# Three sublayers of a perceiver stack: first self attention as two interleaved chains, inverse merges spread over later fills, cross attention values as block diagonal products

## The reference, cut to what matters

```
# sublayer 1, L0_attn: 16 heads of 8; rotary q and k; a cascade over the heads
s[h]   = q[h] @ k[h].T / sqrt(8) + causal
s[h]  += cascade_w[h-1] * mean over the queries of att[h-1]      # h > 0
att[h] = softmax(s[h]);   out = concat(att[h] @ v[h]) @ Wproj

# sublayer 4, L1_attn: a gated delta recurrence, 16 heads of 64, per-channel
# decays a and aR, learned beta and gamma, output clipped, then Wo

# sublayer 9, L3_xattn: q from x; k, v from the context; causal over (32, 257)
lin(x, W, b, A, B) = x @ W.T + b + x @ A.T @ B.T / 16
att = softmax(q @ k.T / sqrt(8) masked to s <= t);  out = lin(att @ v, Wp, bp, Ap, Bp)
```

## Time and profile before

| what | value |
|---|---|
| median of three runs | 3740.51 us (3736.25 to 3745.74) |
| the profiled execution, its own time | 3746.5 us |
| its span, first to last instruction | 3744.7 us, granted clock 0.833 |
| TensorE (PE) busy | 2824.1 us (75%), 50001 matmul records |
| VectorE (DVE) busy | 2288.9 us (61%) |
| ScalarE (ACT), GpSimd (POOL) busy | 1433.9 us (38%), 606.6 us (16%) |

### The profile page before, as it was taken

The page is one execution under the profiler, slowest core; times in us unless marked ns, Lnnn a source line. Parts: engine busy times, 40 slices in busy tenths (PEclk is TensorE's granted clock), DMA queues, the critical chain, the costliest instruction groups (busy, mean ns, idle before and its releaser), DMA issues. The chain is left out here.

```text
span 3744.7 us, 117402 instructions
## 1 busy us (share of the span) xinstructions
PE 2824.1 (75%) x50001; PEld 1980.9 (53%) x50009; DVE 2288.9 (61%) x5777; ACT 1433.9 (38%) x3268; POOL 606.6 (16%) x623
## 2 busy tenths in 40 slices
PE   8852347899995687878787877759998998696654
PEld 5510136444444566666666666536665665384443
DVE  3466532556546887778877887247776555564451
ACT  4312123334333343444444443426665333363220
POOL 0040032455540000000000000000000322061014
PEclk9865567899996698989988998959998998796575
DMA  2100023111101000000000000000001001251013
GB/s 81 40 0 0 0 95 111 55 37 44 43 20 44 3 4 3 4 3 4 4 4 3 4 4 4 3 10 24 24 24 42 0 0 29 71 121 44 5 35 96
DMA packets 69034, 107.01 MB, mean 29 GB/s; under 512 B 10384, under 2 KB 55072, under 8 KB 68032
## 3 DMA queue, kind: packets, MB, share of 16 engines
q1 hardware_dynamic: 56912, 78.25, 6.8%
q0 software_dynamic: 11696, 22.40, 2.4%
HBM read 87.97 MB, written 16.51 MB: 28 GB/s over the span
## 5 line engine op out<-in xcount | busy, mean ns | idle before, releaser
L2885 PE MATMUL psum<-l1d_rw,l1d_cols 64*32 64x32 f32 (+2 forms) x20480 | 246.0, 221 | 115.0 <-issue 71.2
L2394 POOL TENSOR_TENSOR l2x_qx<-l2x_q,consts 128x128 f32<-128x128 f32 x64 | 25.5, 398 | 1723.2 <-DVE l2x_q L2565 1399.5
L2885 PEld LDWEIGHTS psum<-l1d_rw,l1d_cols 64*32 64x32 f32 x20480 | 215.9, 110 | 160.8 <-issue 109.6
L2319 POOL TENSOR_SCALAR l1xs_p<-l1xs_p,l1xs_col 128x257 f32<-128x257 f32 x256 | 238.1, 932 | 243.3 <-DVE l1xs_col L2282 242.7
L2247 ACT ACTIVATE l1xs_p<-psum,l1xs_col 128x257 f32<-128x257 f32 x256 | 122.2, 477 | 256.1 <-DVE l1xs_col L2277 255.9
L2682 ACT COPY l1d_ya<-psum 128x512 f32<-128x512 f32 x160 | 94.2, 589 | 264.4 <-PE psum L2924 264.4
L2277 DVE TENSOR_REDUCE l1xs_col<-psum 128x1 f32<-128x257 f32 x256 | 107.3, 419 | 138.5 <-PE psum L2199 138.5
L3119 DVE TENSOR_TENSOR l1d_rw<-l1d_rw,l1d_tots 128x512 f32<-128x512 f32 x240 | 152.5, 685 | 26.7 <-PE psum L2885 24.9
L2199 PE MATMUL psum<-l1xs_keys,l1xs_qx 128*32 128x257 f32 x2048 | 161.8, 396 | 3.7 <-ACT l1xs_p L2247 3.7
L2211 PE MATMUL psum<-l1xs_pt,l1xs_vals 32*128 32x512 f32 x1152 | 162.0, 637 | 1.3 <-DVE l1xs_pt L2289 1.3
L2824 PE MATMUL psum<-l1d_src,l1d_wp 128*128 128x128 f32 x1024 | 144.2, 300 | 23.3 <-ACT l1d_src L2687 23.3
(11 more groups left out here) (562 smaller groups left out, 7121.1 us busy)
## 6 DMA issues: line engine op xcount, KB each, us to landing
l2f_w<-in_l2f_w SPq DMA_DIRECT2D x16, 768.0 KB, 4.7
l1xs_vals<-in_ctx_strips SPq DMA_DIRECT2D x16, 576.0 KB, 3.8
l0x_ctxT<-in_ctxT SPq DMA_DIRECT2D x16, 516.0 KB, 3.7
l1xs_keys<-in_ctxT SPq DMA_DIRECT2D x16, 516.0 KB, 3.5
l2x_ctxT<-in_ctxT SPq DMA_DIRECT2D x64, 129.0 KB, 2.1
l1d_wp<-in_l1d_wp SPq DMA_DIRECT2D x1, 2048.0 KB, 8.0
l2f_acc<-l2f_zero SPq DMA_DIRECT2D x8, 256.0 KB, 4.5
l2f_sums<-l2f_acc SPq DMA_DIRECT2D x8, 256.0 KB, 5.1
```

The costliest lines, as they stand in the source:

```text
L2319: nc.gpsimd.tensor_scalar(p[:, t % 4, :S2], p[:, t % 4, :S2], col[:, 2, t % 4:t % 4 + 1], None, ALU.mult).then_inc(s["norm"], 1)
L2885: mm = nc.tensor.matmul(k.ps[bank0 + pr + e // per * 2][b * T:b * T + T, e % per * w:(e % per + 1) * w], cols[rr, n, e * 128 + b * T:e * 1 ...
```

## The change

Sublayer 1 becomes one block without loops. The scores are made as in sublayer 9 (16 small products a bank, mask included), the values of a head as a block diagonal stationary tile of 128 rows by 32 columns (`vd`), so that one product does a sequence group. The 16 tiles are cut into two halves x = 0 and 1, each a chain of its own through the heads with instructions of 256 columns; transposes move from VectorE to TensorE; the output weights lie widened (`l0a_wp`, 1 MB instead of 64 KB) with four products per group of four heads. Sublayer 9 takes the same form of values, unit by unit (a unit is a bank of scores), and folds its output weights widened as well (16 more products ahead of the first chunk, 1 MB and 128 KB more to load). In sublayer 4 `turn` only writes the 16 entries that are needed, over a tile that is cleared once, and each merge stands one step later in the round. Computed is the same.

The diff, cut to its core (the old `small_scores` and `small_values` go as a whole):

```
-def small_scores(k, nm, w, scores, rotary, keys_from):
...
@@ -635,101 +427,269 @@
 
 def l0_attn(k):
...
+            def front(c):
+                src = k.XN[:, c * CH:(c + 1) * CH]
+                for n in range(2):
+                    if c > 0:
+                        pe.wait_ge(s["qk"], c * 2 - n)
+                    if c > 0 and n == 1:
+                        pe.wait_ge(s["vd"], c)
+                    for j in range(2):
+                        mm = nc.tensor.matmul(k.ps[pair(c, n) + j][:], wall[:, 2 * n + j, :], src, start=True, stop=True)
+                    mm.then_inc(s["p_mm"], 1)
+                pe.wait_ge(s["qk"], c * 2 + 1)
+                pe.wait_ge(s["group"], c + 1)
+                for b in range(TB):
...
+                                                  qk[r, c % 2, 0, n * T:(n + 1) * T],
+                                                  ks[r, c % 2, n].rearrange("p h s -> p (h s)"), start=False, stop=t == 3)
+                    mm.then_inc(s["sc_mm"], 1)
+
+            def turn(h, x):
+                pe.wait_ge(s["att"], h * 2 + x + 1)
+                if h < H - 1:
+                    nc.tensor.matmul(mean_ps[x][:, :half * T], k.const("meanT"),
+                                     att[:, x, h % 2].rearrange("p n s -> p (n s)"), start=True, stop=True
+                                     ).then_inc(s["mean_mm"], 1)
+                if h * 2 + x > 0:
+                    pe.wait_ge(s["t"], h * 2 + x)
+                for j in range(2):
+                    mm = nc.tensor.transpose(t_ps[:, j * 128:(j + 1) * 128],
+                                             att[:, x, h % 2, 4 * j:4 * j + 4].rearrange("p n s -> p (n s)"),
+                                             k.const("ident"))
+                mm.then_inc(s["t_mm"], 1)
+
+            def values(h, x):
+                pe.wait_ge(s["t"], h * 2 + x + 1)
+                if x == 0 and h % 4 == 0 and h > 0:
+                    pe.wait_ge(s["o"], h // 4)
+                m = slice(32 * (h % 4), 32 * (h % 4) + 32)
+                for j in range(2):
+                    for b in range(TB):
+                        n = (2 * x + j) * TB + b
+                        mm = nc.tensor.matmul(o_ps[m, n * T:(n + 1) * T], vd[:, n, h, :], attT[:, x, j, b * T:(b + 1) * T],
+                                              start=True, stop=True)
+                if x == 1 and h % 4 == 3:
+                    mm.then_inc(s["o_mm"], 1)
+
+            def out(g, t):
+                pe.wait_ge(s["o"], g + 1)
+                if g == 0:
+                    pe.wait_ge(s["kept"], 4 * NCH)
+                mm = nc.tensor.matmul(k.ps[t][:], wp[:, g, t, :], o[:, g % 2, :], start=g == 0, stop=g == 3)
+                if g == 3 or t == 3:
+                    mm.then_inc(s["out_mm"], 1)
+
+            front(0)
+            pe.wait_ge(s["set"], 2)
+            for c in range(1, NCH):
+                front(c)
+                scores(c - 1)
+            scores(NCH - 1)
+            pe.wait_ge(s["vd"], NCH)
+            for h in range(H):
+                turn(h, 0)
+                if h > 0:
+                    values(h - 1, 1)
+                turn(h, 1)
+                values(h, 0)
+                if h >= 4:
+                    out(h // 4 - 1, h % 4)
+            values(H - 1, 1)
+            for t in range(4):
...
+        @block.gpsimd
+        def _(pool):
+            for c in range(NCH):
+                tokens = k.XN[:, c * CH:(c + 1) * CH].rearrange("p (t b s) -> p b t s", t=4, b=TB)
+                nc.gpsimd.tensor_copy(xg[:, c].rearrange("p b (t s) -> p b t s", t=4), tokens).then_inc(s["group"], 1)
...
+            def first(h, x):
+                src = sc[:, h, half * x:half * x + half, :]
+                if h > 0:
+                    dve.wait_ge(s["mean_mm"], (h - 1) * 2 + x + 1)
+                    step(nc.vector.scalar_tensor_tensor(a[:, x].rearrange("p n s -> p (n s)"), mean_ps[x][:, :half * T],
+                                                     cw[:, h:h + 1], src.rearrange("p n s -> p (n s)"), ALU.mult, ALU.add))
+                    src = a[:, x]
+                else:
+                    dve.wait_ge(s["kept"], 8 * x + 8)
+                step(nc.vector.tensor_reduce(mx[:, x], src, AX.X, ALU.max))
+                nc.vector.tensor_tensor(a[:, x], src, spread(mx[:, x]), ALU.subtract).then_inc(s["shift"], 1)
+
+            def second(h, x):
+                dve.wait_ge(s["exp"], h * 2 + x + 1)
+                step(nc.vector.tensor_reduce(rs[:, x], a[:, x], AX.X, ALU.add))
+                step(nc.vector.reciprocal(rs[:, x], rs[:, x]))
+                if h >= 2:
+                    dve.wait_ge(s["t_mm"], (h - 2) * 2 + x + 1)
+                nc.vector.tensor_tensor(att[:, x, h % 2], a[:, x], spread(rs[:, x]), ALU.mult).then_inc(s["att"], 1)
+
...
+                rotate(c)
+            first(0, 0)
+            for h in range(H):
+                if h > 0:
+                    second(h - 1, 1)
+                second(h, 0)
+                first(h, 1)
+                if h + 1 < H:
+                    first(h + 1, 0)
+            second(H - 1, 1)
+            for t in range(4):
...
+            def values(u):
+                c, g = u // 4, u % 4
+                pe.wait_ge(s["at"], u + 1)
+                if g == 0:
+                    pe.wait_ge(s["vd"], c + 1)
                     if c > 0:
...
-                    mm.then_inc(s["own_mm"], 1)
+                        pe.wait_ge(s["o"], c)
+                    else:
+                        pe.wait_ge(s["bias"], 1)
+                for t in range(4):
+                    for h in range(4):
+                        mm = nc.tensor.matmul(o_ps[32 * h:32 * h + 32, g * 128 + t * T:g * 128 + t * T + T],
+                                              vd[:, c % 2, t, 4 * g + h, :], attT[:, u % 2, (t * 4 + h) * T:(t * 4 + h) * T + T],
+                                              start=True, stop=True)
+                mm.then_inc(s["o_mm"], 1)
 
             def out(c):
                 pe.wait_ge(s["o"], c + 1)
-                nc.tensor.matmul(out_ps[:], wf[:, 3, :], o[:], start=True, stop=True).then_inc(s["out_mm"], 1)
-
-            for j, n in enumerate((0, 1, 1, 2)):
+                if c == 0:
+                    pe.wait_ge(s["wide"], 4)
+                    pe.wait_ge(s["bias"], 1)
+                else:
+                    pe.wait_ge(s["x"], c)
+                pe.wait_ge(s["vd"], min(c + 3, NCH))
+                for b in range(TB):
+                    for g in range(4):
...
+                                              o[:, g, :], start=g == 0, stop=g == 3)
+                mm.then_inc(s["out_mm"], 1)
+
+            for j, n in enumerate((0, 1, 1)):
                 mm = nc.tensor.matmul(k.ps[0][:, j * D:(j + 1) * D], wa[:, n, :], wb[:, j, :], start=True, stop=True)
             mm.then_inc(s["fold_mm"], 1)
+            for g in range(4):
+                bank = k.ps[(1, 2, 3, 7)[g]]
+                for b in range(TB):
+                    mm = nc.tensor.matmul(bank[:, b * D:(b + 1) * D], wpa[:, g, b, :], wb[:, 3, :], start=True, stop=True)
+                mm.then_inc(s["wide_mm"], 1)
             pe.wait_ge(s["fold"], 1)
             front(0)
+            rows(0)
             pe.wait_ge(s["set"], 3)
-            for c in range(NCH):
-                scores(c)
-                if c + 1 < NCH:
+            scores(0)
+            pe.wait_ge(s["wide"], 4)
+            scores(1)
+            for g in range(4):
+                mm = nc.tensor.matmul(o_ps[:, :1], wp[:, g, 0, :], bv[:, g:g + 1], start=g == 0, stop=g == 3)
+            mm.then_inc(s["bias_mm"], 1)
+            for u in range(units):
+                c, g = u // 4, u % 4
+                if u + 2 < units:
+                    scores(u + 2)
+                if g == 0 and c + 1 < NCH:
                     front(c + 1)
-                if c > 0:
-                    values(c - 1)
+                if u > 0:
+                    values(u - 1)
+                if g == 1 and c + 1 < NCH:
+                    rows(c + 1)
+                if g == 2 and c > 0:
                     out(c - 1)
-            values(NCH - 1)
+            values(units - 1)
             out(NCH - 1)
...
             def turn(i):
 
                 dve.wait_ge(s["kc"], i + 1)
-                t = Steps(dve, s["turn"], i, 3)
+                t = Steps(dve, s["turn"], i, 2)
+                first = lambda x: x[:, T:T * T:2 * (T + 1)]
                 t(vc.transpose(lt[:, :T * T], kc[:]))
-                t(vc.tensor_scalar(xi[:, :T * T], lt[:, :T * T], -1.0, None, ALU.mult))
-                t(vc.memset(xi[:, 0:T * T:T + 1], 1.0))
+                t(vc.tensor_scalar(first(xi), first(lt), -1.0, None, ALU.mult))
 
             def merge(m):
...
             vc.memset(mr[:], 0.0)
-            vc.memset(ll[:], 0.0).then_inc(s["zero"], 1)
+            vc.memset(ll[:], 0.0)
+            vc.memset(xi[:], 0.0).then_inc(s["zero"], 1)
```

(15 more changed lines are left out.)

523 lines of the change are left out of this document (197 added, 326 removed).

## The result

The changed kernel takes 3516.4 us (median of 4 runs, 3514.4 to 3520.0) against 3743.1 for the kernel before: ratio 0.940, 95% interval 0.938 to 0.942. The forecast was 3556 with a range of 3512 to 3604. The sign, the three places and the order of the terms were right, and the time lies in the range, but not in the likeliest case's own range (3530 to 3580); the nearest case is rival B, 3511, though its parts came out otherwise, as the last sections show.

The account below looks back on a forecast made before the run. It took sublayer 1's heads as one chain, sublayer 4's wait for clip and TensorE's waits for instructions as the bounds; gains of 107 + 58 + 19 = 184 us from 3740.5 gave 3556 us, range 3512 to 3604.

Parts of the forecast that it names:

- the three places: Sublayers 1, 4 and 9 were to gain 107, 58 and 19 us.
- likeliest case: Whole kernel: the forecast itself, 3556 us, own range 3530 to 3580; chance 0.48.
- rival B: Fewer instruction waits or full clock in the heads: sublayers 1, 4, 9 give 130, 74, 25; 3511 us; chance 0.17.
- the order inside the heads: Sublayer 1: chain 0's mean stands behind the output product; chain 1's mean starts at 3.9, chain 0's next at 7.3 us.
- D: Sublayer 1's chains don't overlap: heads about 9.8 us, 37 us more than forecast, 3593 us; chance 0.1.
- what is late next is TensorE itself, and its instructions: Sublayer 4, once the wait for clip goes: 1.3 us a round given back.
- Rival C: Sublayer 4: the wait for clip turns into instruction waits, giving only 20 us; 3594 us; chance 0.2.
- rival E: Sublayer 4: the wait for clip was slack, so only sublayers 1 and 9 gain; 3604 us; chance 0.03.
- some 3 us go again for stretches at full clock: Sublayer 9: taken off the 111 us priced at half clock, giving 108 instead of 127.4.
- sublayer 9 with TensorE 75% busy got 0.55: Sublayer 9's old granted clock, used as evidence against full clock in rival B.
- The rule that fetching is hidden: Sublayer 4: instruction fetch mostly costs nothing, so nothing is given back; 16 us more gain, 3540 us.
- the prediction's own sign, 5 us: Prediction is wrong if a stretch other than the three sublayers moves by more than 5 us.

Follow-up runs that it names:

- run 1: The changed kernel with each output product of sublayer 1's heads issued one place earlier, between the two chains' means of the next head: 3512.7 us, ratio 0.937.
- Runs 5 and 6: run 5, and as 6 the kernel before with only merge_last(0) of sublayer 4 moved right behind clip: 3702.5 us, ratio 0.988.
- run 5: The kernel before with the shortened turn of sublayer 4 alone (16 entries negated instead of 1024, xi filled once): 3734.8 us, ratio 0.997.
- run 3: The changed kernel with sublayer 9's value products cut in four of 8 columns, neighbours in different strips of 32 array columns: 3564.8 us, ratio 0.951.
- run 4: The changed kernel with four stretches of small products that nothing reads put ahead of sublayer 9's folds: 3661.3 us in one profiled execution.
- run 2: The changed kernel with sublayer 9's value products cut in four of 8 columns, four in a row in the same strip: 3585.2 us, ratio 0.957.
- Run 9: run 1's edit plus sublayer 4's table load moved earlier, with TensorE's waits in sublayers 1 and 9 filled with products: 3504.3 us, ratio 0.937 to the kernel before.

## Why the prediction came out as it did

**Right: the three places, and the order inside the heads.** The heads of sublayer 1 came as far apart as forecast, and run 1 shows the cause by moving it. That the period was met to 0.2 us is in part luck, as its two halves were 0.7 too long and 0.5 too short. D is out: the chains overlap. Its price was also wrong: 16 heads at 9.8 us are 157, 50 more than 107 and not 37, which gives 3606, outside the range.

**Right: sublayer 4 waited for `clip`, and time would be given back.** 58 forecast, 54 the usual gain. Runs 5 and 6 put it on the two parts that the prediction named. The gain has the two parts that were forecast: between the two traces before and the six of the new code, TensorE's waits fell by some 36 us (54.8 for `clip` less what was given back), and its products, the same records, took some 22 us less, against 20 forecast for the half clock. The step that failed inside it is who gives back: "what is late next is TensorE itself, and its instructions". Late next was ScalarE with its table load (16.6 us), and `issue` grew by some 10 us in all, not by 18. So the size given back, 18 us, was right with half of its cause. Rival C, 20 us for this sublayer, is out, and by run 5 rival E too. Rival B's 74 is out as well, though the first trace had 68.

**Wrong: the clock in sublayer 9, 20 us.** The failing step is "some 3 us go again for stretches at full clock". With the prices of half clock the sublayer came to 111 us. In the trace the clock is 0.77, not 0.55, and TensorE's work of 75 us fits in 89. The argument against rival B, "sublayer 9 with TensorE 75% busy got 0.55", took the old clock for a property of the sublayer. It belonged to the old value products: run 3, with their old number, gives 32 of 39 us back. That it was their gaps is likely but not shown alone: run 4 has the clock at 0.50 with gaps and at 0.92 without, but run 2 has 0.58 almost without gaps. The prediction had both facts, the gaps of 1.7 us between value groups and the half clock behind a wait of 3.86 us, and did not put them together.

**Wrong in size: sublayer 1, 18 us.** Two terms were off. The front with the first half head took 57.2 us up to the first mean product against 66 + 2.2, 11 us less. It was priced at half clock with 10 us taken off for full clock; with a granted clock of 0.83 that was too little. An estimate from the windows: 45.4 us busy at 0.83 are 75 us of work at 0.50, near the 72.4 of the forecast, so the work was priced right and the clock was not. The other 7 us are one head too many. Between the first mean and the last transposes (229.19 to 328.67) lie 15 periods, and 4 x 5.6 + 11 x 7.3 - 3 = 99.7 us, measured 99.5. The forecast has twelve at 7.3 and the end of 8.3 behind them, but the last head has no mean product that must be waited for, and all that follows its first transposes took 8.8 us. So the heads were not faster than forecast, rival B's 5.3 each was out there, and the total came near B's for other reasons. Run 9 shows what the clock still had to give: 8 us.

**The rule that fetching is hidden** (the Trainium skill, Runtime: NRT & Kernel Launch, section Instruction fetch mechanics) would have given 3540 by the prediction; its own terms, 14 x 1.3 = 18 us, make it 3538. The time came nearer to that than to the forecast for another reason: run 4 speaks against the rule, and what the forecast missed lies in sublayers 1 and 9.

**The unchanged stretches** moved by 0.7 us in the first pair of traces and 12.6 in the second. Single ones moved more in the first pair: between two layer norms with the same code (2870.8 to 3161.2 us before, 2672.8 to 2972.7 changed) 290.5 us became 299.9, and the second trace of the changed kernel has 291.6. So by the prediction's own sign, 5 us, it would be wrong, but the bound was too narrow for this measurement. The layer norms ahead of sublayers 1 and 9 hide the larger loads: from their start to the first product of the sublayer it is 11.9 us instead of 12.4, and 12.2 instead of 11.9.

## What to carry to other kernels

Count TensorE's instructions, not only its columns: where 256 of them did less than about 3.7 us of work here, it starved, and such stretches also had half the clock, so that what stood around them cost more too. Price a dense new stretch at both levels of the clock and give each a chance; the old clock of the stretch is no evidence when its products change. Count the periods of a chain between its first and its last wait, and price its end by itself. Before a difference in a long stretch is explained, compare its waits and its products apart: here the waits repeated within 5 us and the products scattered by 18. In a queue of one engine, put work that nobody waits for (here the output product) into the slot where the engine idles anyway, never ahead of an instruction that another engine waits for.

## What the runs showed of the hardware

- TensorE got 256 instructions per 3.67 us on average (21 groups in 77.0 us, 3.5 to 4.0 each), whether a product had 8 or 32 columns.
- Products of 8 columns took 33 ns a record when four in a row used one strip of 32 array columns (128 in 4.20 us), and 10 to 15 ns when neighbours used different strips (128 in 1.26 us, and 1.90 us at the 1.2 GHz level, which the 4.20 also had).
- A stretch can be busy and slow: in run 2 TensorE was busy 144 of 152 us and its clock was 0.58.
- In the changed kernel TensorE's clock went from 0.99 to 0.50 around a wait of 1.46 us (216.37) and stayed there for 20 us; with two products of 512 columns in that wait it stayed at 1.00 for the scores behind it.
- ScalarE's table load, 1.28 us, started only after the wait ahead of the activation that needed it; one activation of a single column ahead of the wait moved the load into idle time.
- The same code of sublayer 4 took between 1217 and 1243 us in six traces, so differences of 1% there need several traces. The waits were within 5 us of each other; the same 31708 matmul records took 928.8 to 946.6 us.
